# A routed mixture-of-experts stage in parts of 128 rows: eight works of two parts, nine of one with the rows stationary

## The chip, the cores and the metric

One core of a Trainium2 chip runs the whole kernel. The metric is the device time of one launch in microseconds (us), lower is better.

## The reference

A small vision transformer: patch embedding, then two layers of attention and feed-forward, on 32 x 36 = 1152 tokens of 192 features. The change touches the first layer's feed-forward alone, a shared expert for all tokens plus eight routed ones, of which each token takes two:

```
def _expert(xf, W1, W2, W3):                    # 192 -> 768 -> 192
    gate = jnp.minimum(xf @ W1, 10.0)
    up = jnp.clip(xf @ W3, -10.0, 10.0)
    return jax.nn.silu(gate) * up @ W2
scores = jnp.sqrt(jax.nn.softplus(flat @ gate_w))
_, indices = jax.lax.top_k(scores + gate_bias, 2)
weights = take_along_axis(scores, indices); weights /= weights.sum(-1)
y = _expert(flat, w1s, w2s, w3s)                # shared
routed = sum over the two picks of weight * _expert(flat, w1[e], w2[e], w3[e])
```

## The kernel before

**Stages.** Embedding and attention of layer 0 take the first 75 us. Then the shared expert runs in three chunks of 384 tokens (`CHW`), of the third only the first two of six units (`AHEAD`). Now 16 routed works follow, then the rest of the shared expert (the tail, `TAIL`), then layer 1.

**Routing.** VectorE counts each expert's tokens, gives each expert as many works of 256 rows (`WT`) as it needs, and makes a slot for each pick (`bases`, `slots`, L1805 to L1827). GpSimd scatters the rows by indirect DMA into a DRAM array of slots, `marked_rows` (L1479), 18 DMAs. `experts` (L1829) makes the expert number of every work, `eid`, which SyncE loads into a register to address the weights.

**One work.** n counts works; buffers alternate with its parity.

- SyncE loads 1.5 MB of gate and up weights into `stage` (`load_weights`, L375), 0.6 MB of down weights (`load_down`, L384) and 256 rows (`load_rows`, L392). It works through its list in order, each load behind the waits of the ones before it.
- Each fp32 matrix is split into a high and a low part for TensorE's faster format: ScalarE copies the high part of four pieces of 768 columns (L712), then GpSimd subtracts it for three pieces and VectorE for the fourth (`e_split_low`, L728 and L726).
- TensorE transposes the rows (`e_rows`, L701); ScalarE and VectorE split them likewise (L753, L790).
- Gate and up (`e_gate_up`, L665): six units of 128 hidden columns, each 2 matrices x 5 matmuls, the weights stationary and the 256 rows moving. The result has the hidden columns on partitions. ScalarE takes silu (L739), VectorE clips (L760) and multiplies (L767).
- Down (`e_down`, L685): two tiles of 128 rows, six fp32 matmuls each (two instructions per matmul), the hidden values stationary. VectorE copies the tile out (`e_copy`, L805) and GpSimd scatters it home to DRAM, `slots_out` (`send_home`, L1489).

**Order.** Every engine has its own list, written out by hand. TensorE: gate and up of n, row transposes of n+1, down of n-1. GpSimd:

```
for n in range(3, WORKS + 1):
    if n > 4:
        pool.wait_ge(st_y[n % 2], 16 * (n - 4 + n % 2))
    e_split_low(nc.gpsimd, pool, n, n % 2, range(3))
    pool.wait_ge(S0["w_lo"], 4 * n + 3)
    if n > 3:
        send_home(n - 3)
```

The wait on `st_y` is for the landing of the send of work n-4, the one issued at the end of the turn before. When all works are home, SyncE loads them back in token order (`G`, L412), VectorE adds them weighted (L1894), and layer 1's first projection begins (L1074).

Of the kernel before, what the change touches and what calls it, by code (L numbers as in the profile page):

```python
# [5 lines left out]
F32 = mybir.dt.float32  # L6
# [32 lines left out]
WT = 256  # L39

WORKS = (PICKS * TOK - E0) // WT + E0
SLOTS = WORKS * WT
# [11 lines left out]
ZROWS = SLOTS // P // 4  # L54
SPARE = P * ZROWS

# [6 lines left out]
TAIL_AT = ((6, 0), (6, 1), (7, 0))  # L63
TAIL_ADD = ((6, 8, 6), (8, 9, 7))
# [81 lines left out]
def tower(nc, patches, tokw, consts, rows, wa, l1w, wo, moe0w, moe0d, moe1w, xs, ys, out):  # L146
    xs = nc.dram_tensor("marked_rows", (SLOTS, XW1), F32, kind="Internal").ap()
    ys = ys.rearrange("w s d -> (w s) d")
    with ExitStack() as ctx:
# [57 lines left out]
        base = sb("base", [P, E0])  # L207
        slot = sb("slot", [P, TILES * E0])
# [4 lines left out]
        eidf = sb("eidf", [P, WORKS])  # L213
        eid = sb("eid", [P, WORKS], I32)

# [3 lines left out]
        with r1a:  # L219
# [8 lines left out]
            XR = [sb(f"XR{b}", [P, WT // P, 256 + 1], F32, r1a) for b in range(4)]  # L228
            XWh = [sb(f"XWh{b}", [P, 2 * WT], F32R, r1a) for b in range(2)]
            XWl = [sb(f"XWl{b}", [P, 2 * WT], F32R, r1a) for b in range(2)]  # L230
            YO = [sb(f"YO{b}", [P, WT // P, D], F32, r1a) for b in range(2)]
# [65 lines left out]
        r_own, r_sel, r_pos, r_idx, r_eid = (sem("r_" + s) for s in ("own", "sel", "pos", "idx", "eid"))  # L297
        zeroed, zero_set, scattered = sem("zeroed"), sem("zero_set"), sem("scattered")
        ld_w2 = [sem(f"ld_w2{b}") for b in range(2)]
        ld_x = [sem(f"ld_x{b}") for b in range(4)]  # L300
# [36 lines left out]

        block = ctx.enter_context(nc.Block())
# [4 lines left out]
        def _(sp):  # L343
# [17 lines left out]
            for j in range(4):  # L361
                sp.dma_start(xz[:, j * ZROWS * XW1:(j + 1) * ZROWS * XW1],
                             zero[:].rearrange("p r d -> p (r d)")).then_inc(zeroed, 16)
# [4 lines left out]
            def load_weights(n):  # L368
# [5 lines left out]
                experts[n] = sp.value_load(eid[0:1, n - 1:n], min_val=1, max_val=E0)  # L374
# [3 lines left out]
            def load_down(n):  # L378
                if n >= 2:
                    sp.wait_ge(S["down_ready"], 9 + 2 * (n - 2))  # L380
# [6 lines left out]
            def load_rows(n):  # L387
                if n > 4:
                    sp.wait_ge(x_T, n - 4)
                    sp.wait_ge(st_y[n % 2], 16 * (n - 4 + n % 2))  # L390
                rows = xs[(n - 1) * WT:n * WT, :].rearrange("(a p) d -> p a d", p=P)
                sp.dma_start(XR[n % 4][:, :, 0:D], rows[:, :, 0:D]).then_inc(ld_x[n % 4], 16)  # L392
                sp.dma_start(XR[n % 4][:, :, D:256 + 1], rows[:, :, P:XW1]).then_inc(ld_x[n % 4], 16)
# [12 lines left out]
            load_down(TAIL)  # L406
            for par in range(2):
                sp.wait_ge(st_y[par], 16 * WORKS)
# [213 lines left out]
        def units(n):  # L622

            return (n + 1) * FC0 + AHEAD

        TAIL_U = units(TAIL) - AHEAD
        TAIL_D = 9 + 2 * WORKS

        def e_operands(n, c, w, cols):
# [5 lines left out]
            else:  # L635
                h, l = XWh[n], XWl[n]
                xpart = [h[:, 0:WT], h[:, 0:WT], l[:, 0:WT], h[:, WT:2 * WT], l[:, WT:2 * WT]]
# [8 lines left out]
        def e_gate_up(pe, u, n, par, c, these=range(MOE0.fc)):  # L646

            width = WT if c is None else CHW
# [4 lines left out]
            for fc in these:  # L653
                if c is not None or (isinstance(n, int) and n == 1 and fc < 2):
                    if not (isinstance(u, int) and u == 0 and fc < 2):
                        pe.wait_ge(S0["silu_ready"], u + (fc - 1))
                elif not (isinstance(n, int) and n == 1 and fc == 2):
                    pe.wait_ge(S0["h_ready"], u + (fc - 2))
                if not (isinstance(u, int) and u == 0 and fc < 2):
# [8 lines left out]
        def e_down(pe, u, qpar, n, par, shared, loaded, these=range(MOE0.fc)):  # L668
# [1552 lines left out]
```

## Time and profile before

| | us |
|---|---|
| median of 3 runs | 566.83 |
| lowest, highest | 561.97, 567.05 |
| span of the profiled execution | 564.3 |

The profile covers one execution; its own time is its span, 564.3 us, 2.5 us under the median. Times inside it count from the span's start. A row of a timeline or chain gives start, duration and what ran; "[x <-y]" behind it is idle time ahead of it and what ended it. Busy time of TensorE (PE) is no measure of its peak: matmuls overlap, so the pitch from one start to the next is what counts, not the mean duration.

### The profile page before, as it was taken

Reading aid. Unit: us, or ns where it says so; the run is one execution under the profiler, and the core shown is the slowest. Engines: PE = TensorE matmul, PEld = TensorE weight load, DVE = VectorE, ACT = ScalarE, POOL = GpSimd, SP = SyncE. Lnnn points to the kernel's source line nnn. Section 1 sums busy time; section 2 is a strip of 40 time slices with the busy share of each in tenths; the row PEclk is TensorE's granted clock in tenths of the full one; section 3 lists DMA queues with packets and bytes.
Section 4 is the critical chain, followed back from the end, with each engine's and each line's share of the span. In section 5 each row is a group of like instructions: output and inputs, shape, how many; then the busy total and the mean of one; then the engine's idle time right before and its main releaser. Section 6 shows DMA issues by size and latency. Waiting matters only on the chain.

```text
span 564.3 us, 9739 instructions
## 1 busy us (share of the span) xinstructions
PE 518.0 (92%) x3430; PEld 493.6 (87%) x3430; DVE 376.2 (67%) x892; ACT 256.7 (45%) x531; POOL 230.4 (41%) x194
## 2 busy tenths in 40 slices
PE   5799896989999999999999979998996889999996
PEld 5798895989999999999999869786775789999995
DVE  1665848756666666656664587699977765566665
ACT  0337463315544555445543234984750463254331
POOL 1403100746566577656766313486743100041200
PEclk9999959899999999999999989999798799899998
DMA  8750000847465676557662503000201000000001
GB/s 337 259 227 1 2 0 1 314 126 258 144 235 199 225 257 249 196 201 255 216 253 76 189 3 153 2 2 1 77 1 51 28 0 2 2 0 2 1 21 43
DMA packets 22634, 65.03 MB, mean 115 GB/s; under 512 B 6432, under 2 KB 15008, under 8 KB 19776
## 3 DMA queue, kind: packets, MB, share of 16 engines
q1 hardware_dynamic: 20192, 59.55, 29.9%
q0 software_dynamic: 2400, 4.93, 2.5%
q8 instruction: 25, 0.41, 0.3%
q14 instruction: 17, 0.14, 0.1%
HBM read 55.50 MB, written 8.97 MB: 114 GB/s over the span
## 4 chain that ended last, share of the span: by engine, by line
PE 56%; DVE 10%; DMA 4%; POOL 4%; issue 3%; ACT 2%; SPq 0%; DVEq 0%; POOLq 0%; ACTq 0%
PE psum L665 17%; PE psum L448 10%; PE psum L685 10%; PE psum L1074 4%; PE psum L465 4%; PE psum L1106 3%; PE psum L1089 2%; PE psum L472 2%; DMA slots_out<-YO,XR 2%; PE psum L1131 2%; DMA XR<-marked_rows 1%; POOL w0l L728 1%; PE psum L701 1%; POOL w0t L726 1%; DVE OW L2009 1%
## 5 line engine op out<-in xcount | busy, mean ns | idle before, releaser
L728 POOL TENSOR_TENSOR w0l<-stage,w0h 128x768 fp32r<-128x768 f32 x34 | 62.5, 1839 | 81.9 <-ACT w0h L712 69.6
L685 PE MATMUL psum<-w0d,a0h 128*128 128x192 f32 x492 | 84.7, 331 | 1.3 <-DVE a0h L767 1.3
L685 PEld LDWEIGHTS psum<-w0d,a0h 128*128 128x128 f32 x492 | 81.2, 193 | 1.6 <-DVE a0h L767 1.6
L760 DVE TENSOR_SCALAR a0t<-psum 128x256 f32<-128x256 f32 (+1 forms) x114 | 50.8, 445 | 42.6 <-PE psum L665 42.4
L739 ACT ACTIVATE psum<-psum 128x256 f32<-128x256 f32 x96 | 35.3, 368 | 85.3 <-PE psum L665 81.3
L665 PE MATMUL psum<-XWh,w0h 128*128 128x256 f32 x192 | 56.1, 292 | 0.0
L665 PE MATMUL psum<-XWh,w0t 128*128 128x256 f32 x192 | 54.4, 283 | 0.0
L665 PE MATMUL psum<-XWl,w0h 128*128 128x256 f32 x192 | 53.9, 281 | 0.0
L665 PE MATMUL psum<-XWl,w0t 128*128 128x256 f32 x192 | 53.9, 281 | 0.0
L665 PE MATMUL psum<-XWh,w0l 128*128 128x256 f32 x192 | 53.8, 280 | 0.0
L448 PE MATMUL psum<-X,w1h 128*128 128x384 f32 x144 | 50.1, 348 | 1.5 <-DVE a1hf L603 1.5
L767 DVE SCALAR_TENSOR_TENSOR a0h<-psum,a0t 128x256 f32<-128x256 f32 x96 | 40.8, 425 | 10.0
L543 ACT ACTIVATE a1s<-psum 128x384 f32<-128x384 f32 x36 | 17.6, 491 | 55.2 <-PE psum L448 55.2
L726 POOL TENSOR_TENSOR w0t<-stage,w0t 64x768 fp32r<-64x768 f32 x20 | 36.8, 1839 | 9.7 <-ACT w0t L712 7.1
L603 DVE TENSOR_TENSOR a1hf<-psum,a1s 128x384 f32<-128x384 f32 x36 | 20.0, 557 | 28.9 <-ACT a1s L543 28.8
L465 PE MATMUL psum<-d,a1hh 128*128 128x384 f32 x108 | 35.2, 385 | 3.2 <-DVE a1hl L567 1.9
L448 PE MATMUL psum<-X,w1t 128*128 128x384 f32 x144 | 37.6, 342 | 0.0
L665 PEld LDWEIGHTS psum<-XWh,w0h 128*128 128x128 f32 x192 | 36.3, 189 | 0.0
L665 PEld LDWEIGHTS psum<-XWh,w0t 128*128 128x128 f32 x192 | 36.2, 189 | 0.0
L665 PEld LDWEIGHTS psum<-XWh,w0l 128*128 128x128 f32 x192 | 36.1, 188 | 0.0
L665 PEld LDWEIGHTS psum<-XWl,w0h 128*128 128x128 f32 x192 | 36.1, 188 | 0.0
L665 PEld LDWEIGHTS psum<-XWl,w0t 128*128 128x128 f32 x192 | 36.1, 188 | 0.0
(261 smaller groups left out, 1290.8 us busy)
## 6 DMA issues: line engine op xcount, KB each, us to landing
stage<-moe0w SPq DMA_DIRECT2D x18, 1536.0 KB, 7.2
w0d<-moe0d SPq DMA_DIRECT2D x18, 576.0 KB, 3.9
stage<-moe1w SPq DMA_DIRECT2D x4, 1056.0 KB, 4.9
marked_rows<-zero SPq DMA_DIRECT2D x4, 772.0 KB, 13.1
patch<-patches SPq DMA_DIRECT2D x4, 768.0 KB, 8.1
XR<-marked_rows SPq DMA_DIRECT2D x16, 192.0 KB, 3.5
G<-slots_out SPq DMA_DIRECT2D x6, 288.0 KB, 4.4
XR<-marked_rows SPq DMA_DIRECT2D x16, 65.0 KB, 3.7
```

Of the source, the lines that this page charges most:

```text
L448: last = nc.tensor.matmul(bank[bk][:, 0:CHW], wt, x, start=(i == 0), stop=(i == 4))
L465: return nc.tensor.matmul(bank[4 + d % 4][:, 0:2 * D], A["hh"][q][:, fc, cols], w["d"][:, fc, :, :].rearrange("p a d -> p (a d)"), start=( ...
L543: nc.scalar.activation(A["s"][par][:], bank[par][:, 0:CHW], ACT.Silu).then_inc(S["silu_ready"], 1)
L603: nc.vector.tensor_tensor(A["hf"][par][:], bank[2 + par][:, 0:CHW], A["s"][par][:], ALU.mult).then_inc(S["h_ready"], 1)
L665: last = nc.tensor.matmul(bank[b][:, 0:width], w, x, start=(i == 0), stop=(i == 4))
L685: last = nc.tensor.matmul(dst, A0["h"][qpar][:, fc, t * P:(t + 1) * P], W0[par]["down"][:, fc, :], start=(fc == these[0]), stop=(fc == the ...
L726: ins = engine.tensor_tensor(dst, src[64:P], dst.bitcast(F32), ALU.subtract)
L728: ins = engine.tensor_tensor(W0[par]["l"][:, mat, :], src, W0[par]["h"][:, mat, :].bitcast(F32), ALU.subtract)
L739: nc.scalar.activation(e_silu(fc, width, routed), bank[gate_bank(fc, routed)][:, 0:width], ACT.Silu).then_inc(S0["silu_ready"], 1)
L760: nc.vector.tensor_scalar(A0["t"][fc % 2][:, 0:width], bank[2 + fc % 2][:, 0:width], LIMIT, -LIMIT, ALU.min, ALU.max).then_inc(S0["clip_re ...
L767: nc.vector.scalar_tensor_tensor(out=A0["h"][qpar][:, fc, 0:width], in0=e_silu(fc, width, width == WT), scalar=SILU_LIMIT, in1=A0["t"][fc ...
L1074: last = nc.tensor.matmul(bank[(2 * g + half) % 6][0:GW, 0:L1H], x, w, start=(i == 0), stop=(i == 4))
```

## The change

The routed rows are cut into parts of 128 (`PARTS` is 25). Even works (`WIDE`, eight) take two parts of one expert as before, odd works (`LONE`, nine) take one; they alternate, lone first, 17 works in all. A lone work keeps its rows stationary and streams the weights in halves of 384 columns (`e_rows_gate_up`); what comes out has rows on partitions, so TensorE turns it in two sets of three transposes (`e_turn`), which ScalarE copies out (`e_turned`). GpSimd splits all four pieces of a lone work and two of a wide one, VectorE the other two. Weights are loaded two works ahead. VectorE makes the expert and the first part of each work (`wide_parts`, `lone_parts`, `experts`, `places`), and SyncE loads the part number into a register too (`part`, with the semaphore `r_part`). The loops over works are unrolled.

```
-WT = 256
-WORKS = (PICKS * TOK - E0) // WT + E0
+WT = P
+PARTS = (PICKS * TOK - E0) // WT + E0
+WIDE = E0
+LONE = PARTS - 2 * WIDE
+WORKS = WIDE + LONE
...
             load_weights(1)
             load_down(1)
             load_weights(2)
+            load_weights(3)
+            sp.wait_ge(r_part, 1)
             sp.wait_ge(scattered, 16 * PICKS * TILES)
             load_rows(1)
             load_rows(2)
+            load_down(2)
             for n in range(2, WORKS + 1):
-                if n > 2:
-                    load_rows(n)
-                load_weights(n + 1)
-                load_down(n)
+                if n < WORKS:
+                    load_rows(n + 1)
+                if n + 2 <= TAIL:
+                    load_weights(n + 2)
+                load_down(n + 1)
...
+        def e_rows_gate_up(pe, u, n):
+            pe.wait_ge(x_lo, n)
+            for half in range(2):
...
+                for mat in range(2):
+                    pe.wait_ge(S0["w_lo"], n * 4 + 2 * (mat + 1))
+                    for i, (x, w) in enumerate(e_operands(1, None, W0[1], (slice(0, P), mat,
+                                                                           slice(half * LH, (half + 1) * LH)))):
+                        last = nc.tensor.matmul(bank[2 * mat + half][:, 0:LH], x, w, start=(i == 0), stop=(i == 4))
+                last.then_inc(S0["gu_ready"], 1)
+
+        def e_turn(pe, u, n, half):
+            pe.wait_ge(S0["h_ready"], u + (half + 1))
+            if half:
+                pe.wait_ge(h_out, turned_in(n) - 1)
+            for k in range(3):
+                last = nc.tensor.transpose(bank[7][:, k * P:(k + 1) * P], hR[:, half * LH + k * P:half * LH + (k + 1) * P],
+                                           ident)
+            last.then_inc(h_T, 1)
...
+            for n in range(1, WORKS + 1):                      # TensorE
+                u = units(n)
+                if n % 2:
+                    e_rows_gate_up(pe, u, n)
+                    if n < WORKS:
+                        e_rows(pe, n + 1)
+                    e_turn(pe, u, n, 0)
+                    if n > 1:
+                        e_down(pe, units(n - 1), 0, n - 1, 0, False, loaded(n - 1))
+                        e_turn(pe, u, n, 1)
                 else:
+                    e_gate_up(pe, u, n, 0, None, range(1))
+                    if n == 2:
+                        e_turn(pe, units(1), 1, 1)
+                    e_gate_up(pe, u, n, 0, None, range(1, FC0))
+                    e_rows(pe, n + 1)
+                    e_down(pe, units(n - 1), 1, n - 1, 1, False, loaded(n - 1))
+            e_gate_up(pe, TAIL_U, TAIL, 0, 2, range(AHEAD, AHEAD + 1))
+            e_down(pe, units(WORKS), 1, WORKS, 1, False, loaded(WORKS))
+            e_gate_up(pe, TAIL_U, TAIL, 0, 2, range(AHEAD + 1, FC0))
+            e_down(pe, TAIL_U, 0, TAIL, 0, True, loaded(TAIL), range(AHEAD, FC0))
...
+            for n in range(1, WORKS + 1):                      # ScalarE
+                u = units(n)
+                if n % 2:
+                    if n > 1:
+                        e_split_next(act, n + 1, 0)
+                        e_split_next(act, n + 1, 1)
+                    e_rows_silu(act, u, 0)
+                    if n > 1:
+                        e_split_next(act, n + 1, 2)
+                    e_rows_silu(act, u, 1)
+                    if n > 1:
+                        e_split_next(act, n + 1, 3)
+                    if n < WORKS:
+                        e_rows_high(act, n + 1, units(n))
+                    e_turned(act, n, 0)
+                    if n > 1:
+                        e_turned(act, n, 1)
+                else:
+                    if n > 2:
+                        e_split_next(act, n + 1, 0)
+                    e_act(act, u, 2 * WT, these=range(1))
+                    if n == 2:
+                        e_turned(act, 1, 1)
+                        e_split_next(act, 3, 0)
+                    for fc in range(1, FC0):
+                        e_split_next(act, n + 1, fc) if fc < 4 else None
+                        e_act(act, u, 2 * WT, these=range(fc, fc + 1))
+                    e_rows_high(act, n + 1, units(n))
...
-            for n in range(3, WORKS + 1):
+            for n in range(3, TAIL + 1):                       # GpSimd
                 if n > 4:
-                    pool.wait_ge(st_y[n % 2], 16 * (n - 4 + n % 2))
-                e_split_low(nc.gpsimd, pool, n, n % 2, range(3))
-                pool.wait_ge(S0["w_lo"], 4 * n + 3)
+                    pool.wait_ge(st_y[n % 2], sent(n - 4))
+                parts = 4 if n % 2 else 2
+                e_split_low(nc.gpsimd, pool, n, n % 2, range(parts))
+                pool.wait_ge(S0["w_lo"], 4 * n + parts)
                 if n > 3:
                     send_home(n - 3)
...
-            experts()
             e_product(dve, 0, 0, 5, CHW)
-            e_dve(dve, FC0, 1, CHW, None, None, None)
+            e_dve(dve, FC0, 1, CHW, None, {1: wide_parts, 2: lone_parts, 3: experts})
             e_split_low(nc.vector, dve, 1, 1)
+            places()
             prior()
             share(sc, E0, comb[:], True)
             weights()
...
+            e_rows_low(dve, 1)
+            e_split_low(nc.vector, dve, 2, 0, (0, 1))
...
+            for n in range(1, WORKS + 1):                      # VectorE
+                u = units(n)
+                if n % 2:
+                    if n > 2:
+                        dve.wait_ge(h_T, turned_in(n - 2))
...
+                    for half in range(2):
+                        e_rows_product(dve, u, half)
+                else:
+                    e_dve(dve, u, 0, 2 * WT, downs(n - 2))
+                if n < WORKS:
+                    e_rows_low(dve, n + 1)
+                if n % 2 and n > 1:
+                    e_split_low(nc.vector, dve, n + 1, 0, (2, 3))
+                if n > 1:
+                    e_copy(dve, n - 1)
+            e_dve(dve, TAIL_U, 0, CHW, downs(WORKS - 1), these=range(AHEAD, FC0 - 1))
+            e_copy(dve, WORKS)
+            e_dve(dve, TAIL_U, 0, CHW, None, these=range(FC0 - 1, FC0))
```

## Rows read from the trace of the kernel before

**Rows 1.** The page's engine shares: busy time, share of span, instructions.

```profile
PE 518.0 (92%) x3430; PEld 493.6 (87%) x3430; DVE 376.2 (67%) x892; ACT 256.7 (45%) x531; POOL 230.4 (41%) x194
```

**Rows 2.** The chain that ended last, steady stretch: start, us, what ran.

```profile
202.24 3.90 PE psum L685 x24
206.15 7.12 PE psum L665 x60
213.26 0.44 PE psum L701 x4
```

**Rows 3.** Busy time by stretch: engines, TensorE's clock, DMA share, GB/s.

```profile
148.80:298.10 149.30, 149.17 (x1146) 148.97 (x1145) 97.03 (x208) 75.58 (x143) 97.58 (x66) 1.00 0.65 229
```

**Rows 4.** GpSimd's timeline through one work.

```profile
208.62 1.84 POOL L728 TENSOR_TENSOR w0l<-stage,w0h 128x768 fp32r<-128x768 f32 x1 [3.14 <-ACT w0h L712]
...
212.60 1.83 POOL L728 TENSOR_TENSOR w0l<-stage,w0h 128x768 fp32r<-128x768 f32 x1
214.71 0.99 POOL L1489 DMA_INDIRECT slots_out<-YO,XR  x1 [0.28 <-POOL w0l L728]
216.00 0.96 POOL L1489 DMA_INDIRECT slots_out<-YO,XR  x1 [0.31 <-issue]
```

**Rows 5.** The chain in layer 1: ten matmuls, rows stationary, 396 columns moving.

```profile
336.21 1.80 PE psum L1074 x10
```

**Rows 6.** Landings: all sends; those of 297.8, 299.1; SyncE there; scatter of 101.7.

```profile
slots_out<-YO,XR POOLq DMA_INDIRECT x32, 2.3
...
L1489 POOL DMA_INDIRECT slots_out<-YO,XR x2: 957/958/959, 297.8 to 299.1; - x2
...
DMA to landing us min/median/max: 4.3/4.4/4.6
...
298.35 0.36 SPq L384 DMA_DIRECT2D w0d<-moe0d  x1
...
DMA to landing us min/median/max: 7.0/7.0/7.0
```

**Rows 7.** SyncE's timeline: one steady turn, the first weight load, its landing.

```profile
206.31 0.36 SPq L384 DMA_DIRECT2D w0d<-moe0d  x1
...
208.56 0.35 SPq L375 DMA_DIRECT2D stage<-moe0w  x1
...
99.97 0.35 SPq L375 DMA_DIRECT2D stage<-moe0w  x1
...
DMA to landing us min/median/max: 8.6/8.6/8.6
```

**Rows 8.** VectorE's timeline in the opening: expert numbers, first and last split, what follows.

```profile
98.77 0.17 DVE L1837 TENSOR_SCALAR eid<-eidf 128x16 int32<-128x16 f32 x1
...
103.08 0.56 DVE L760 TENSOR_SCALAR a0t<-psum 128x384 f32<-128x384 f32 x1 [1.40 <-PE psum L665]
...
109.58 0.96 DVE L728 TENSOR_TENSOR w0l<-stage,w0h 128x768 fp32r<-128x768 f32 x1
...
112.76 0.97 DVE L726 TENSOR_TENSOR w0t<-stage,w0t 64x768 fp32r<-64x768 f32 x1
...
117.50 1.02 DVE L796 TENSOR_TENSOR H<-psum,H 128x384 f32<-128x384 f32 x2
```

**Rows 9.** ScalarE's timeline in a work: one weight copy.

```profile
207.65 0.84 ACT L712 ACTIVATE w0h<-stage 128x768 fp32r<-128x768 f32 x1
```

**Rows 10.** TensorE before work 1: timeline, clock of that stretch, chain to work 2.

```profile
125.57 0.66 PE L701 MATMUL psum<-const,XR 128*128 128x128 f32 x4 [2.08 <-DMA XR<-marked_rows]
...
126.20:129.60 3.40, 3.40 (x14) 3.40 (x12) 1.25 (x2) 3.33 (x5) 1.82 (x1) 0.50 0.95 309
...
133.85 10.68 PE psum L665 x90
```

**Rows 11.** The chain at the end: last send, first projection of layer 1.

```profile
315.23 2.32 DMA slots_out<-YO,XR
330.18 5.37 PE psum L1074 x20
```

More of the change, by code:

```diff
@@ L207, in tower @@
         base = sb("base", [P, E0])
+        twos = sb("twos", [P, E0])
+        rest = sb("rest", [P, E0])
+        ends = sb("ends", [P, 2, 2, E0])
+        shift2 = sb("shift2", [P, 2, E0])
+        order = sb("order", [P, 2, LONE])
+        place = sb("place", [P, 2, LONE])
+        held = sb("held", [P, 2, LONE])
+        part = sb("part", [P, 2, LONE], I32)
         slot = sb("slot", [P, TILES * E0])
@@ L296, in tower @@
         rt1_z, rt1_b, rt1_p = sem("rt1_z"), sem("rt1_b"), sem("rt1_p")
-        r_own, r_sel, r_pos, r_idx, r_eid = (sem("r_" + s) for s in ("own", "sel", "pos", "idx", "eid"))
+        r_own, r_sel, r_pos, r_idx, r_eid, r_part = (sem("r_" + s) for s in ("own", "sel", "pos", "idx", "eid", "part"))
         zeroed, zero_set, scattered = sem("zeroed"), sem("zero_set"), sem("scattered")
         ld_w2 = [sem(f"ld_w2{b}") for b in range(2)]
-        ld_x = [sem(f"ld_x{b}") for b in range(4)]
+        ld_x = [[sem(f"ld_x{b}{i}") for i in range(RING3)] for b in range(2)]
+        h_T, h_out = sem("h_T"), sem("h_out")
         marked, copied, numbered = sem("marked"), sem("copied"), sem("numbered")
@@ L679, in e_down @@
                     dst = bank[e_bank(t)][:, 0:D]
[L680 removed]
+                    if n == 1:
                         pe.wait_ge(S0["acc_done"], len(SHARED_ADD))
[L682 to L683 removed]
+                    elif t == 0:
+                        pe.wait_ge(y_done, copies(n - 1) if n % 2 == 0 else copies(n - 2) + 1)
+                    elif n > 2:
+                        pe.wait_ge(y_done, copies(n - 2))
                 for fc in these:
[L685 removed]
+                    h = hT[:, fc, :] if lone else A0["h"][qpar][:, fc, t * P:(t + 1) * P]
+                    last = nc.tensor.matmul(dst, h, W0[par]["down"][:, fc, :],
                                             start=(fc == these[0]), stop=(fc == these[-1]))
@@ new lines, in _, with reached @@
+            lone_to, wide_to, lone_from, wide_from = (ends[:, i, k, :] for i in range(2) for k in range(2))
+            grid = [P, 2, LONE, E0]
+            def reached(to, side):
+                return nc.vector.tensor_tensor(
+                    to.rearrange("p (k w e) -> p k w e", k=2, e=E0),
+                    counts[:, 0:LONE].unsqueeze(1).unsqueeze(3).to_broadcast(grid),
+                    ends[:, side].unsqueeze(2).to_broadcast(grid), ALU.is_ge)
+            above, within = (rk[i][:, 0:2 * LONE * E0] for i in range(2))
@@ new lines, in wide_parts, with lone_parts @@
+            def wide_parts():
+                k0 = rk[0][:, 0:E0 * FULL].rearrange("p (e k) -> p e k", k=FULL)
+                own.link(nc.vector.tensor_reduce(twos[:], k0[:, :, 1:FULL:2], AX.X, ALU.add))
+                earlier(wide_from, twos[:])
+                own.link(nc.vector.tensor_tensor(wide_to, wide_from, twos[:], ALU.add))
+                own.link(nc.vector.tensor_scalar(ends[:, :, 1, :], ends[:, :, 1, :], float(WIDE), None, ALU.min))
+            def lone_parts():
+                own.link(nc.vector.tensor_tensor(twos[:], wide_to, wide_from, ALU.subtract))
+                own.link(nc.vector.scalar_tensor_tensor(out=rest[:], in0=twos[:], scalar=-2.0, in1=works[:],
+                                                        op0=ALU.mult, op1=ALU.add))
+                earlier(lone_from, rest[:])
+                own.link(nc.vector.tensor_tensor(lone_to, lone_from, rest[:], ALU.add))
```

304 lines of the change are left out of this document (160 added, 144 removed).

## The prediction

> **What bounds the kernel now.** I read the page's engine shares first, then the chain of waits, then the timelines of the routed stretch engine by engine. The page says TensorE is busy 92% of the span and GpSimd 41% [rows 1]; those are averages, and the change touches only the stretch from about 125 to 330 us. There the chain repeats one pattern: 7.12 us of gate/up matmuls (60 of them, one every 0.119 us), 0.44 us for four transposes, 3.90 us of down matmuls (24 instructions, 0.163 us each), then the next work: 11.46 us in all [rows 2]. Over 148.8 to 298.1 us TensorE never rests and its granted clock is 1.00, its 2.4 GHz level [rows 3]. So today a routed work costs 11.46 us, and a pair 22.92 us, all TensorE.
>
> The second thing to see is how little room GpSimd has. Its three weight splits start 1.99 us apart (208.62 to 212.60 in two steps) and run 1.83 us, the first send starts 0.28 us after them, the second 1.29 us later, and this second send lands 2.3 us after it starts [rows 4]. Before its next splits GpSimd waits for exactly that landing (the wait on st_y for work n-4, whose send stands right before it). One work therefore needs 3 x 1.99 + 0.12 + 1.29 + 2.3 = 9.7 us on GpSimd, of 11.46. It waits for ScalarE's copy only in the remainder.
>
> **TensorE's own sum.** A lone work has 2 halves x 2 matrices x 5 matmuls, 20 with 384 moving columns. The nearest row, also rows stationary and weights moving (396 columns), is ten in 1.80 us [rows 5]; I take 0.176 us each, 3.5 us. Its two row transposes are 0.22 us, its six turning transposes 0.66 us, its one down tile 1.95 us. A wide work stays 11.46 us. A pair is 11.46 + 3.5 + 0.22 + 0.66 + 1.95 = 17.8 us against 22.92: 5.1 us less for each of eight pairs, 41 us in all, less about 6 us for the seventeenth work. If TensorE stayed the bound this would be the gain. It won't stay the bound.
>
> **GpSimd's sum.** The weights of 17 works and the tail must still be split, whatever the number of rows. In a pair GpSimd takes four pieces of the lone work, two sends of the wide one, the wait for their landing, two pieces of the next wide work, one send, and its landing. From the first piece: last piece ends at 3 x 1.99 + 1.83 = 7.80; second send starts at 7.80 + 0.28 + 1.29 = 9.37; it lands L2 later; two pieces 3.82; the single send starts 0.28 later, at 13.57 + L2; it lands L1 later; 0.1 to restart. The loop is 13.67 + L1 + L2. With both at 2.3 it is 18.3 us, already above TensorE's 17.8. The same loop passes through VectorE: the wide work's pieces 2 and 3 wait there for GpSimd's two, 1.06 us each (four from 109.58 to 113.73) [rows 8], and TensorE's wide work waits for them. In the lone phase TensorE now waits some 2 to 4 us in each pair.
>
> **What the sends land in is the disputed price.** Before, sends mostly go out with no load starting: 2.3 us. Two didn't. Those of 297.8 and 299.1 us stand 0.55 us before and 0.73 us after SyncE's down load of 298.35, and landed in 4.6 and 4.3 us; and a scatter of 101.7 us, with 1.5 MB weight loads queued, took 7.0 [rows 6]. After the change, the lone work's fourth piece ends 8 to 10 us after the wide work's first matmul (call that G). The two sends go out at about G+9 and G+10. SyncE issues the next down load when the lone down matmuls end, at G + 7.12 + 0.22 + 1.95 = G+9.3: the spacing of the 4.3 and 4.6 rows. I take L2 = 4.5 (ends 2.3 and 7.0). The single send goes out near G+19. The wide work's down matmuls end at G+17.5, which releases another down load; the weight load before it is issued at G+12.4 (SyncE's turn from down load to weight load lasts 2.3 us [rows 7], the new register load adds some 0.7) and takes 7 us. I take L1 = 3.4, the middle of 2.3 and 4.6. So a pair is 13.67 + 4.5 + 3.4 = 21.6 us, only 1.3 below before.
>
> **Other engines in a pair.** ScalarE: eight copies of 0.84 [rows 9], eight silus, two turned copies and two row copies, none over 0.6: about 12 us. VectorE: eight clip and product pairs of some 1 us, two splits and five copies, about 12 us. Both hide. Behind VectorE's wait for GpSimd's pieces stand the copies of the wide work before; their send comes half a pair later, so that costs nothing. The weights arrive 7 us after SyncE's issue and are wanted 7 us or more after it; 5 MB in 21.6 us is 230 GB/s, what rows 3 already show. The turn's waits (h_T, h_out) stand behind down matmuls of 3.90 us and cost nothing; without that cover each would cost 0.5 us of ScalarE copy.
>
> **The opening.** The expert numbers move from before VectorE's last product of chunk 0 (98.8 us) to behind the fourth unit of chunk 1. VectorE's idle of 1.4 us ahead of the third unit [rows 8] hides wide_parts (five instructions of about 0.2), lone_parts makes the next clip 0.6 late, experts follow at about 106.5: eid at 107.4 instead of 98.9. SyncE's load takes 1.0 us to issue and 8.6 to land [rows 7]: 117.0. VectorE's four splits of work 1 then end at 122.1 instead of 113.7 [rows 8]. Behind them on VectorE queue places (eleven small instructions, 2.9 us, to 125.0), prior, share and weights (3.75, from 113.73 to 117.50 before; to 128.8), three additions (1.6, to 130.4) and two clip and product pairs of chunk 2 (2.3, to 132.7). Rows of work 1 need r_part and a register load, and stand behind the load of work 3 that SyncE now issues first, so they land about 131, when the third addition also frees the bank. TensorE's down matmuls of chunk 2 start at 132.8 and take 3.8 (before they had the 1.2 GHz level, granted clock 0.50, after an idle of 2.1 us [rows 10]; now the idle is some 7). The lone work runs 136.6 to 140.1; silu, product and row split (0.3 + 0.5 + 0.56 + 0.69) let work 2 start at 142.3. Before it started at 133.85 + 3.56 = 137.4 [rows 10]: 4.9 us lost. I can't bound this tightly: 0 to 8.
>
> **The first pair** has no send to wait for: TensorE's 17.8 plus 0.95 because ScalarE's second copy for work 3 stands behind silu and the turned copy. 18.75 us.
>
> **The closing.** The tail's first unit waits for the eighteenth split. Then one unit 1.75, down of work 17 1.95, two units 3.5, the product 1.38 behind them, and only then the copy of work 17 (0.36), since VectorE's order puts it behind three tail units: 8.95. Before, the last send starts at 315.23 and the first projection of layer 1 at 330.18 [rows 11], 14.95 later. Together 24.0 us. The half clock after TensorE's stall adds 1.7 (four units, 3.4 us at half rate). What follows 330.18 is the same as before.
>
> **The sum.** Work 2 at 142.3, the first pair 18.75, seven pairs of 21.6 = 151.2 (the seventh ends where the tail starts), closing 24.0 + 1.7: 337.95 us, against 330.18, so 7.8 us later. The profiled span of 564.3 becomes 572.1. The listed runs' median is 2.5 above that span; I carry this excess over: 574.6.
>
> On the half clock: the row of 126.2 to 129.6 us shows 0.50 after a 2.1 us idle [rows 10]. In each pair TensorE would idle as long, so the clock will fall there too. It costs nothing while GpSimd is the bound. The Trainium skill ("TensorE: Matmul & The Clock Gate", HAM oscillation) warns of just such a loop, a wait per iteration that brings the clock down each time; the trace of before has no such loop and can't show it. By that rule each stall would cost TensorE up to 1.7 us, which changes the sum only where TensorE is the bound.
>
> **Rivals.** *Sends land free.* If the landings stay 2.3, the loop is 18.3 and the pair TensorE's 18.75. 142.3 + 8 x 18.75 + 24.0 = 316.3, 13.9 earlier: 552.9. For it: the median of all 32 sends is 2.3 us. Against it: the two that met a fresh load [rows 6]. It decides at a pair of 20.5, where the time equals that of before. The Trainium skill ("DMA: Bandwidth & Descriptors", queues, rings and completion order) says that each DMA engine goes round-robin between queue rows and switches at packet boundaries. By that with small packets a send would hardly be held, and this rival's 552.9 would come out; with a load's whole share as one packet it would wait the load out, which the 4.6 us row looks like. *Only the wide sends are held.* L1 = 2.3 and L2 = 4.5 is that pair of 20.5: 142.3 + 18.75 + 7 x 20.5 + 25.7 = 330.2, no change, 566.8. *A send waits out a whole 1.5 MB load.* L2 = 7.0 as the scatter, pair 24.1: 355.4, 25 later, 592. Against it: the weight load is issued at G+12.4, after the sends, unless GpSimd runs late.
>
> **How the numbers follow.** Forecast 0.40 (568 to 580 by its ends of the opening and L1); wide sends only 0.20 (561 to 569); free 0.27 (549 to 558); whole load 0.11; something else 0.02. Within 1% (5.7 us, about what a measurement of this kernel can tell from no change) fall 0.2 and a quarter of the forecast's: 0.29. Faster 0.29, slower 0.42. The range takes in the free case and stops short of the last: 551 to 586. The forecast's own range is 568 to 580.
>
> **What would show it.** Wide works starting 21 to 22 us apart; GpSimd's splits waiting on slots_out; sends landing at 4 to 5 us; TensorE idle 2 to 4 us before each wide work, with the granted clock below 1; lone gate/up in 3.5 us; work 2 near 142; last send some 9 us behind the tail's first matmul. Pairs of 18.8 with sends at 2.3 would prove me wrong.

## The result and the profile after

The changed kernel takes 582.1 us (median of four runs, 580.1 to 583.8) against 564.5 for the kernel before: ratio 1.031, interval 1.027 to 1.036. Forecast was 574.6, slower, inside 551 to 586: the sign was right, the loss of 7.8 us was 17.6. Of the almost 10 us between the two losses, 7.5 are the changed kernel's; the other 2.4 come from the kernel before, whose median with a fourth run is 564.5 and not 566.8. Some runs come out a few per cent longer; the ratios, here and in the table of experiments, leave these out and compare with runs of the kernel before made beside them, so they are not quotients of the medians shown. The profiled execution has a span of 580.2 us and lies 0.1 us from its median; its sum below can be laid beside the forecast's term by term.

The chain of waits, from work 2 to work 4 and on (start, us, what). It answers to rows 2.

```profile
141.56 1.43 PE psum L727 x10
...
153.07 3.48 DMA XR<-marked_rows
156.55 0.04 issue
156.60 0.66 PE psum L798 x4
157.25 0.33 PE psum L752 x3
157.58 3.90 PE psum L780 x24
161.48 0.33 PE psum L752 x3
161.81 3.53 PE psum L727 x30
...
173.15 3.22 DMA XR<-marked_rows
...
177.40 3.90 PE psum L780 x24
181.31 0.33 PE psum L752 x3
181.63 3.88 issue
185.52 9.51 PE psum L727 x60
```

Where one kind of step was repeated without a gap before [rows 2], two holes stand now. The row transposes of the next wide work (L798) wait for rows that are still in flight, and before four of the seven wide gate/ups from work 4 to work 16 (those of works 6, 10, 12 and 16) TensorE is idle for 0.5 to 5.2 us, called issue. That name says only that the profile has no releaser. GpSimd's timeline of the same stretch has it:

```profile
170.26 1.83 POOL L826 TENSOR_TENSOR w0t<-stage,w0t 64x768 fp32r<-64x768 f32 x1
172.37 0.99 POOL L1614 DMA_INDIRECT homes<-YO,XR  x1 [0.28 <-POOL w0t L826]
173.66 0.96 POOL L1614 DMA_INDIRECT homes<-YO,XR  x1 [0.30 <-issue]
179.54 1.80 POOL L828 TENSOR_TENSOR w0l<-stage,w0h 128x768 fp32r<-128x768 f32 x1 [4.92 <-DMA homes<-YO,XR]
181.49 1.80 POOL L826 TENSOR_TENSOR w0t<-stage,w0t 64x768 fp32r<-64x768 f32 x1
183.57 1.64 POOL L1614 DMA_INDIRECT homes<-YO,XR  x1 [0.28 <-POOL w0t L826]
```

The second wide send starts at 173.66 and GpSimd goes on 5.88 us later. VectorE's two differences for the same work wait for GpSimd's two:

```profile
183.39 0.96 DVE L828 TENSOR_TENSOR w0l<-stage,w0h 128x768 fp32r<-128x768 f32 x1 [4.96 <-POOL w0t L826]
184.46 0.96 DVE L826 TENSOR_TENSOR w0t<-stage,w0t 64x768 fp32r<-64x768 f32 x1
```

TensorE starts at 185.52, behind them. From the start of the second send to its next difference GpSimd takes 5.9, 4.6, 4.4, 7.0, 4.9, 4.2 and 3.1 us in the seven pairs, mean 4.9; six single sends land 3.0 to 4.6 us after they start, mean 3.5. The waits between 160 and 300 us (line waited for: us in total, times, longest) and the stretches (PE, PEld, DVE, ACT, POOL busy, granted clock, DMA share, GB/s):

```profile
POOL w0l L828 <- DMA homes<-YO,XR: 34.0, 10, 6.0
PEld psum L798 <- DMA XR<-marked_rows: 12.5, 6, 2.7
```

```profile
181.63:185.52 3.89, 0.01 (x2) 0.04 (x1) 1.99 (x3) 1.33 (x2) 3.30 (x2) 0.79 0.60 186
185.52:195.03 9.51, 9.51 (x62) 9.51 (x63) 4.79 (x12) 4.09 (x8) 7.18 (x4) 0.73 0.49 177
161.81:317.81 156.00, 130.79 (x893) 126.11 (x892) 77.14 (x160) 76.28 (x140) 101.78 (x63) 0.95 0.65 218
```

Against [rows 3], TensorE is busy 130.8 of 156.0 us instead of all of it: 3.6 us idle in each pair, where the forecast said 2 to 4. In two of the seven wide gate/ups, behind idle times of 3.9 and 5.2 us, the granted clock is 0.73 and the matmuls take 9.5 us instead of 7.1. The end, against [rows 11]:

```profile
317.81 3.57 PE psum L727 x10
321.38 3.23 PE psum L780 x12
324.61 3.51 PE psum L727 x20
...
329.28 0.36 DVE YO L920
...
330.39 2.33 DMA homes<-YO,XR
...
345.68 4.59 PE psum L1181 x13
```

### The profile page after: what moved, and what is told of

The parts are those of the page before. It is cut to its first block, busy times and chain, and to the rows that moved or that the text cites. A ratio compares the mean times of both kernels' runs of the same rounds, so it can differ in the third digit from the quotient of the medians.

```text
span 580.2 us, 8867 instructions
## 1 busy us (share of the span) xinstructions
PE 495.6 (85%) x3086; PEld 463.8 (80%) x3086; DVE 354.6 (61%) x852; ACT 255.7 (44%) x524; POOL 226.5 (39%) x187
## 4 chain that ended last, share of the span: by engine, by line
PE 65%; DVE 14%; DMA 8%; issue 6%; ACT 4%; SPq 2%; POOL 1%; DVEq 0%; POOLq 0%; ACTq 0%
PE psum L727 14%; PE psum L780 11%; PE psum L505 10%; DMA XR<-marked_rows 4%; PE psum L1181 4%; PE psum L522 3%; PE psum L947 3%; PE psum L1196 3%; PE psum L1213 3%; PE psum L968 2%; PE psum L1028 2%; PE psum L1238 2%; PE psum L529 2%; DVE Y L1731 1%; DMA stage<-moe0w 1%
## 5 line engine op out<-in xcount | busy, mean ns | idle before, releaser
L600 ACT ACTIVATE a1s<-psum 128x384 f32<-128x384 f32 x36 | 17.6, 490 | 54.7 <-PE psum L505 54.7
L727 PE MATMUL psum<-XWh,w0h 128*128 128x256 f32 x96 | 29.0, 302 | 12.2 <-issue 11.0
L809 ACT ACTIVATE w0h<-stage 128x768 fp32r<-128x768 f32 x38 | 31.9, 839 | 11.0 <-DMA stage<-moe0w 10.8
L1614 POOL DMA_INDIRECT homes<-YO,XR x25 | 29.0, 1159 | 17.2 <-DVE YO L920 10.6
L727 PE MATMUL psum<-X,w0h 128*128 128x384 f32 x72 | 28.7, 399 | 7.7 <-DVE w0t L826 2.9
L1213 PEld LDWEIGHTS psum<-VW,AT 108*108 108x108 f32 x264 | 28.9, 184 | 5.4 <-issue 4.7
L1196 PE MATMUL psum<-XB 96*108 96x432 f32 (+1 forms) x88 | 30.0, 487 | 2.6 <-DVE AT L2206 2.6
L809 ACT ACTIVATE w0t<-stage 128x768 fp32r<-128x768 f32 x38 | 31.7, 835 | 0.0
L839 ACT ACTIVATE psum<-psum 128x256 f32<-128x256 f32 x48 | 17.6, 367 | 29.2 <-PE psum L727 28.9
L727 PEld LDWEIGHTS psum<-XWh,w0h 128*128 128x128 f32 x96 | 19.4, 202 | 13.6 <-issue 12.2
L1213 PE MATMUL psum<-VW,AT 108*108 108x112 f32 (+2 forms) x264 | 29.0, 269 | 0.9 <-issue 0.9
```

Of the source, the lines that this page charges most:

```text
L727: last = nc.tensor.matmul(bank[b][:, 0:width], w, x, start=(i == 0), stop=(i == 4))
L809: nc.scalar.activation(W0[par]["t" if two else "h"][:, mat, :], W0[par]["stage"][:, (2 * mat + two) * F0:(2 * mat + two + 1) * F0], ACT.Co ...
L839: nc.scalar.activation(e_silu(fc, width, routed), bank[gate_bank(fc, routed)][:, 0:width], ACT.Silu).then_inc(S0["silu_ready"], 1)
L1196: last = nc.tensor.matmul(bank[b][0:GW, at * GW:(at + c1 - c0) * GW], kT1[g % 2][:, half, :], qT1[g % 2][:, half, c0:c1, :].rearrange("p c ...
L1213: last = nc.tensor.matmul(bank[1 + h // HH][0:GW, h % HH * 3 * HD:h % HH * 3 * HD + n], AT[g % 2][:, h, :], VW[g // 2 % 2][:].rearrange("p ...
L1614: nc.gpsimd.indirect_dma_start(out=ys, out_offset=bass.IndirectOffsetOnAxis(ap=to[:, t, 256:257].bitcast(I32), axis=0), in_=YO[n % 2][:, t ...
```

## Experiments

Below, "first pair" is from work 2's first gate/up matmul to work 4's, "pair" the mean of the seven from there to the tail's, both from TensorE's timeline. In the changed kernel they are 20.0 and 22.3 us (20.25 and 22.3 by the chain, which begins work 4 at 161.81). "Tail to last send" is the time from the tail's first matmul to the start of the last send. Theory 1 says that GpSimd's waits for landings set the pair; theory 2 that the late rows do.

| run | us | ratio to before, interval | work 2 | first pair | pair | tail to last send |
|---|---|---|---|---|---|---|
| changed | 582.1 | 1.031 [1.027, 1.036] | 141.6 | 20.0 | 22.3 | 12.6 |
| again_changed (one run) | 578.0 | – | 140.6 | 19.9 | 22.5 | 9.8 |
| e1_piece0_first | 565.5 | 1.005 [1.000, 1.010] | 143.9 | 20.3 | 20.1 | 9.8 |
| e2_rows_early | 584.0 | 1.036 [1.028, 1.045] | 145.0 | 18.7 | 23.3 | 9.8 |
| e3_both | 563.0 | 1.000 [0.995, 1.005] | 141.5 | 18.7 | 20.5 | 9.8 |
| e4_no_down_loads | 560.2 | 0.995 [0.989, 1.000] | 145.8 | 18.9 | 19.6 | 9.8 |
| e5_copy_sooner | 578.0 | 1.021 [1.015, 1.026] | 143.4 | 19.8 | 22.6 | 6.8 |
| e6_rows_first | 579.9 | 1.027 [1.020, 1.034] | 140.0 | 19.9 | 22.5 | 11.2 |
| e8_four_edits_and_order | 562.8 | 0.994 [0.990, 0.998] | 139.2 | 18.7 | 21.0 | 5.2 |
| e9_vector_takes_64 | 552.8 | 0.978 [0.972, 0.985] | 139.5 | 20.1 | 19.2 | 5.2 |
| e10_loads_behind | 580.4 | 1.030 [1.022, 1.038] | 139.9 | 19.9 | 23.3 | 9.8 |
| e11_spread_differences | 540.2 | 0.960 [0.956, 0.965] | 137.3 | 19.2 | 18.6 | 5.2 |
| e12_swap_alone | 560.8 | 0.997 [0.993, 1.000] | 138.4 | 21.4 | 20.0 | 9.7 |

**e1_piece0_first.** GpSimd's loop:

```diff
+                parts = 4 if n % 2 else 2
+                e_split_low(nc.gpsimd, pool, n, n % 2, range(1))
                 if n > 4:
                     pool.wait_ge(st_y[n % 2], sent(n - 4))
-                parts = 4 if n % 2 else 2
-                e_split_low(nc.gpsimd, pool, n, n % 2, range(parts))
+                e_split_low(nc.gpsimd, pool, n, n % 2, range(1, parts))
```

> GpSimd's wait for the landing of its sends stands behind its first difference of 128 partitions instead of before it, so 1.80 us of work goes under each of the waits. Theory 1 (the landings set the pair: 13.67 us of GpSimd's work plus two waits): up to 1.8 us less for each of the 16 waits after work 1, a pair of 19.5 to 20.5 us instead of 22.3, the program 12 to 25 us below the 582.1 of the changed kernel. Theory 2 (the rows of the next wide work, issued behind the down load in SyncE's list, set it, TensorE's pair 19.9 us): the wide works already start at 19.9 to 22.3 us, so at most the part above 19.9 goes, and nothing if the down load alone sets it: 0 to 3 us less.

16.6 us less for one wait moved behind one instruction; by the two profiles 15.4 of it lies in the seven pairs. GpSimd's timeline there:

```profile
194.84 0.96 POOL L1614 DMA_INDIRECT homes<-YO,XR  x1 [0.30 <-issue]
195.86 1.82 POOL L828 TENSOR_TENSOR w0l<-stage,w0h 128x768 fp32r<-128x768 f32 x1
200.47 1.81 POOL L826 TENSOR_TENSOR w0t<-stage,w0t 64x768 fp32r<-64x768 f32 x1 [2.78 <-DMA homes<-YO,XR]
```

The send takes as long to land as before, but 1.8 us of it is covered; of the 34.0 us of waits 11.3 are left in the same window. The wait is kept ahead of GpSimd's differences of 64 partitions; the first of 128 now runs beside the transfer. Neither kind reads or writes what is sent, and no run drops the wait with the work left on GpSimd, so whether it could go altogether isn't shown. Theory 1 holds as the cause of the pair of 22.3. The pair stops at 20.1 us, which is TensorE's sum with the wait for rows (17.8 + 2), and the chain between 184 and 226 us runs through the row loads at each turn. So theory 2 names what comes next; e3 shows that it isn't alone there.

**e2_rows_early.** SyncE's list, rows loaded two works ahead:

```diff
+            load_rows(3)
             load_down(2)
             for n in range(2, WORKS + 1):
-                if n < WORKS:
-                    load_rows(n + 1)
+                if n + 2 <= WORKS:
+                    load_rows(n + 2)
```

> Rows of work 3 are loaded up front and in the loop those of two works ahead, so they land before the row transposes need them; GpSimd's waits stay. Theory 2 (late rows set the pair): TensorE's stop of 2 us before the row transposes of a wide work goes and with it up to 2 us a pair, 10 to 16 us in all. Theory 1 (GpSimd's waits set it): the stop moves from before the row transposes to before gate and up, the pair stays at 22.3 and the time within 3 us of 582.1.

No gain. No wait for rows is left in the steady stretch, and the first pair, which has no landing to wait for, falls to 18.7: the forecast's 18.75. In the others the idle moves to before gate/up (GpSimd still waits 38.2 us in 10 times). Theory 2 is right for the first pair and wrong for the rest.

**e3_both.** Both edits.

> The first two edits together. Theory 1: as the first alone, 12 to 25 us below 582.1, with a further 0 to 3 us. If both walls stand close to each other (TensorE with late rows 19.9, GpSimd 21 to 22): the first alone stops at a pair of 19.9, both together reach 18 to 19, so that the two together give 5 to 8 us more than the first alone.

563.0, first pair 18.7, but the pair is 20.5, not 18 to 19. GpSimd still waits for landings (15.0 us in 8 times), and ScalarE waits longer for stage loads (20.3 us in 11, against 9.0 in 7). Early rows brought nothing beyond the first pair: with them away, the chain runs through a stage load of 9.3 us and through idle times of 2.8 to 3.6 us before the wide gate/up.

**e4_no_down_loads.** Down weights from work 3 on aren't reloaded (4 of 1536 columns are moved), so this run leaves out a part of the work:

```diff
+                cols = 4 if n > 2 else MOE0.fc * D
-                sp.dma_start(W0[n % 2]["down"].rearrange("p a b -> p (a b)"), ...
+                sp.dma_start(W0[n % 2]["down"].rearrange("p a b -> p (a b)")[:, 0:cols], ...
```

> Leaves out the reload of the down weights from work 3 on (4 columns of 1536 are moved, all waits stay). If these 0.75 MB transfers are what GpSimd's sends queue with, the landings of the wide works' second sends fall from 4 to 7 us to 2.3 to 3.0, two landings a pair together from about 8.2 to 5.3, and under theory 1 the pair falls by about 2.5 to 3 us and the program by 18 to 25 us. If the stage loads (1.5 MB) are what they meet, the landings stay at 4 to 7 us and the program within 5 us of 582.1; rows then also land sooner only by the time of the down load before them.

With the waits in their old places the pair falls by 2.7 us:

```profile
POOL w0l L829 <- DMA homes<-YO,XR: 21.2, 12, 2.1
```

A wait is 1.8 us instead of 3.4, and from the start of a wide work's second send GpSimd goes on after 2.9 us on average (2.4 to 3.1) instead of 4.9. So the down load is what makes a good part of the landings long, as the forecast read from the two sends at 297.8 and 299.1 [rows 6]. (The down load is 0.56 MB, not the 0.75 that the expectation says.) Rows land sooner too, in 2.5 us instead of 3.5, so part of the gain may be theirs.

**e5_copy_sooner.** VectorE's end:

```diff
-            e_dve(dve, TAIL_U, 0, CHW, downs(WORKS - 1), these=range(AHEAD, FC0 - 1))
+            e_dve(dve, TAIL_U, 0, CHW, downs(WORKS - 1), these=range(AHEAD, AHEAD + 1))
             e_copy(dve, WORKS)
-            e_dve(dve, TAIL_U, 0, CHW, None, these=range(FC0 - 1, FC0))
+            e_dve(dve, TAIL_U, 0, CHW, None, these=range(AHEAD + 1, FC0))
```

> Only the closing: VectorE copies the last work's rows (line 920) behind the first of the tail's units instead of behind three of them. If the copy's place in VectorE's list sets the last send, the stretch from the tail's start to the last send's issue falls from 12.6 us to 7 to 9 and the program by 4 to 5 us to 577 to 578. If it is the tail's own work at half clock that sets the end, the send goes out sooner and the first projection of the next layer starts as long after the tail's start as before (27.9 us): 582.

578.0, in the expected range. The last send goes out 6.8 us behind the tail's start (12.6), with the down matmuls partly at the low clock again (granted clock 0.70):

```profile
321.14 2.54 PE psum L727 x10
323.68 3.08 PE psum L780 x12
...
326.85 0.37 DVE YO L920
...
327.97 2.33 DMA homes<-YO,XR
...
343.04 2.28 PE psum L1181 x6
```

From the tail to layer 1 it is 21.9 us instead of 27.9. Not all of that shows in the total, since in this execution the tail begins 3.3 us later. Nor is all of it the edit's. The changed kernel's second execution, without an edit, has the full clock there (start, us, what):

```profile
317.88 2.02 PE psum L727 x10
319.90 1.95 PE psum L780 x12
321.85 3.51 PE psum L727 x20
...
342.70 2.61 PE psum L1181 x7
```

That is 24.8 us from the tail to layer 1, as in six other profiles with the old order (24.8 to 24.9), and 20.1 to 20.3 in e8, e9 and e11, which have this edit and the full clock. The place of the copy is worth 4.6 us; the rest belongs to the clock of one execution.

**e6_rows_first.** `load_weights(3)` moves behind `load_rows(2)` in SyncE's opening.

> Only the opening: SyncE issues the third stage load behind the rows of works 1 and 2 instead of ahead of them. If that 1.5 MB load is what makes work 1 late, work 2 starts 1 to 3 us before the 141.56 of the changed kernel and the program is at 578 to 582; if the expert numbers and the shared expert's last matmuls set it, nothing changes (582), and the lone work 3 gets its weights later: up to 585.

Work 2 at 140.0, 1.6 us sooner, and 579.9. e5, whose opening is the changed kernel's (143.4), and the changed kernel's second execution (140.6) say that a microsecond or two of work 2's start is scatter: what this edit brings isn't shown.

**e8_four_edits_and_order.** e3, e5, e6, and in SyncE's loop `load_weights(n + 2)` ahead of `load_rows(n + 2)`.

> The first two edits, the sooner copy, the later third stage load, and in SyncE's loop the stage load ahead of the rows (rows are loaded a work earlier, so they can wait). With the first two alone the pair is 20.2 us (141.47 to 303.34) and the chain's new step is the stage load, issued 3.0 us after the down matmuls that free the down buffer. If the load's late issue is the wall, the pair falls to 18.6 to 19.5 us, and with the closing's 5 us the program reaches 545 to 555; if GpSimd's landings are still the wall, the pair stays at 20 and the program at 556 to 562.

562.8. The closing keeps its gain (5.2 us to the last send), the pair doesn't fall (21.0). The load's late issue wasn't the wall; GpSimd waits for landings 19.3 us in 6 times.

**e9_vector_takes_64.** Besides, the 64-partition differences go to VectorE:

```diff
-                parts = 4 if n % 2 else 2
-                e_split_low(nc.gpsimd, pool, n, n % 2, range(1))
-                if n > 4:
-                    pool.wait_ge(st_y[n % 2], sent(n - 4))
-                e_split_low(nc.gpsimd, pool, n, n % 2, range(1, parts))
-                pool.wait_ge(S0["w_lo"], 4 * n + parts)
+                e_split_low(nc.gpsimd, pool, n, n % 2, (0, 2))
+                pool.wait_ge(S0["w_lo"], 4 * n + 3)
...
                         e_rows_product(dve, u, half)
+                        if half == 0 and n > 1:
+                            e_split_low(nc.vector, dve, n + 1, 0, (1,))
...
-                    e_dve(dve, u, 0, 2 * WT, downs(n - 2))
+                    t_part = lambda i, n=n: e_split_low(nc.vector, dve, n + 1, 1, (i,))
+                    e_dve(dve, u, 0, 2 * WT, downs(n - 2),
+                          {1: lambda: t_part(1), 5: lambda: t_part(3)} if n < WORKS else {})
...
-                    e_split_low(nc.vector, dve, n + 1, 0, (2, 3))
+                    e_split_low(nc.vector, dve, n + 1, 0, (3,))
```

> As the one before, and VectorE makes all differences of 64 partitions (0.96 us each there, 1.84 on GpSimd), GpSimd those of 128. GpSimd then has four differences and three sends a pair (about 12 us) and waits for no landing at all. If GpSimd and its landings are the wall, TensorE's own sum becomes it: a pair of 17.8 to 18.5 us, 535 to 547 for the program. If the stage loads (9 us from issue to landing and 5 to 8 us of splitting for each of two buffers) are the wall, the pair stays at 18.5 to 20 and this run gives within 3 us what the one before gives. If VectorE's two more differences delay its products, the wide gate and up get longer than 7.1 us.

No landing is waited for, and the pair falls to 19.2: 552.8, 2.2% under the kernel before. Two things in its trace can keep it above TensorE's 17.8: VectorE's extra 0.96 us makes the wide gate/up 7.7 to 8.8 us long, and a lone work's stage buffer goes round in 18.7 (load 9.35, last difference 9.2 behind its landing).

**e12_swap_alone.** The changed kernel with only that exchange, its rows, opening and closing as they were.

> The changed kernel with one edit: VectorE makes the differences of 64 partitions and GpSimd those of 128, so GpSimd waits for no landing. Rows, copy and opening stay as they were. Theory 1 with the late rows as the next wall (TensorE's sum with the wait for rows 19.8 to 19.9 us a pair): pair 19.9 to 20.5 and 558 to 565 for the program. If the landings alone were the wall and the rows hide: the pair of the version with all edits, 19.1, and 555 to 558.

560.8, pair 20.0: 17.8, rows 1.4, and the longer gate/up. One exchange of engines is worth 21 us and brings the program level with before. In the profiles, 22.5 us apart, 15 of it lie in the eight pairs; work 2 starts 3.2 us sooner, which this edit doesn't touch, and the closing is 3.1 us shorter, as it is in the changed kernel's second execution.

**e10_loads_behind.** In the opening, `load_weights(2)` stands behind `load_rows(1)` and `load_weights(3)` behind `load_rows(2)`.

> Only the opening: the second stage load too is issued behind the rows of work 1, so that 2.1 MB instead of 3.6 or 5.2 MB are in flight from 105 us on. In the changed kernel TensorE's down matmuls of the shared expert stop for 0.3 to 2.1 us again and again from 109 to 120 us and end at 129, while the loads run. If the amount in flight makes these stops, they end by about 114 us, the down matmuls end by 122 and the rows of work 1 land sooner by the same 2 to 4 us; work 2 then waits for its own stage load (issued at about 121, landed 130, split by 136 to 138) and starts at 137 to 140 instead of 141.56, 576 to 580 for the program. If the stops have another cause they stay, and work 2 starts at 140 to 144.

TensorE's stops at 109 to 120 us are gone (busy 10.00 us of the 10 between 109 and 119), and work 2 starts at 139.9. By itself this points to the loads in flight. But e12 and e11, with as many in flight (390 and 382 GB/s), have no stops either.

**again_changed.** No edit.

> The changed kernel once more, unedited. TensorE's stops at 109 to 120 us stood in seven profiles of it and its variants (3.2 to 5.9 us busy of the 10 between 109 and 119) and not in three (10.00 of 10), two of which have the same loads in flight. If they belong to the program, they stand here in the same place (TensorE busy 3 to 5 us of those 10) and work 2 starts at 141 to 142; if they belong to the single execution, they may be missing, and work 2 then starts 2 to 4 us sooner. The pairs stay at 22 to 22.7 us, the landings at 3 to 7.

The same window in the two executions of the same program:

```profile
109.00:119.00 10.00, 3.94 (x10) 1.64 (x8) 5.48 (x10) 3.53 (x5) 6.45 (x7) 0.66 0.95 379
```

```profile
109.00:119.00 10.00, 10.00 (x64) 10.00 (x63) 2.50 (x4) 3.04 (x4) 7.63 (x8) 1.00 1.00 363
```

The stops belong to the execution. (The expectation counts seven profiles with them; by the same window there are nine: the changed kernel's first and those of e1 to e9.) The tail starts at 317.9 in one and 317.8 in the other, so they don't explain the loss. What causes them stays open.

**e11_spread_differences.** e9, with the two differences between a clip and its product:

```diff
-                          {1: lambda: t_part(1), 5: lambda: t_part(3)} if n < WORKS else {})
+                          mid={2: lambda: t_part(1), 4: lambda: t_part(3)} if n < WORKS else {})
```

> The fastest version so far (pair 19.1 us, 552.8) with VectorE's two differences for a lone work placed between a clip and its product (third and fifth unit) instead of behind a product (second and sixth). The lone works' stage buffer goes round in 18.7 us there (load 9.3, then the last difference 9.2 us after its landing, behind the sixth unit), and the wide gate and up takes 7.7 to 8.8 us instead of 7.1. If these two set the pair, it falls by about 1 us to 18.0 to 18.5 and the program to 544 to 549; if something else does, it stays within 2 us of 552.8.

540.2 us, 4.0% under the kernel before, the fastest here. VectorE's timeline and the routed stretch:

```profile
198.04 0.42 DVE L871 TENSOR_SCALAR a0t<-psum 128x256 f32<-128x256 f32 x1
198.49 0.96 DVE L827 TENSOR_TENSOR w0t<-stage,w0t 64x768 fp32r<-64x768 f32 x1
199.48 0.42 DVE L878 SCALAR_TENSOR_TENSOR a0h<-psum,a0t 128x256 f32<-128x256 f32 x1
```

```profile
156.55:286.54 129.99, 127.40 (x895) 123.29 (x894) 88.56 (x175) 74.32 (x139) 81.12 (x49) 1.00 0.73 257
```

TensorE's next unit waits for the clip of this unit, which frees its PSUM bank, but for the product of the unit before only, so the product can wait. The pair is 18.6, 0.6 us less and not the expected 1, TensorE is busy 127.4 of 130.0 us at the full clock, and GpSimd falls from 101.8 to 81.1 us. Of the 11.0 us between the spans of e9 and e11, 7.5 lie before the tail. 2.1 of them lie before work 2, where e9 has the stops of 109 to 120 us and e11 has not; 5.4 lie in the eight pairs, and only these can be put down to the edit. The other 3.5 lie behind the tail, where both have the same code, and aren't explained.

## Why the prediction was right in its sign and short in its size

The terms add up: 7.7 us too little at the first projection of layer 1 (345.68 against 337.95), 0.4 behind it. Two of the forecast's own sums are rounded up by 0.1 to 0.15 us: work 2 adds up to 142.15 and the closing without the clock to 23.9.

| term | forecast | measured | difference |
|---|---|---|---|
| work 2 starts | 142.3 | 141.56 | -0.7 |
| first pair | 18.75 | 20.25 | +1.5 |
| seven pairs | 151.2 | 156.0 | +4.8 |
| closing | 25.7 | 27.87 | +2.2 |

**TensorE's own sum** had its lone gate/up right (3.49 to 3.53 us for 20) and missed a step. The half-length lone phase pulled the rows of the next wide work, which stand behind the down load in SyncE's list, into TensorE's path: down load, register load, two row loads, landing 3.5 us after issue, 2 us of idle. The sum with rows is 19.9, not 17.8. That is the first pair's 1.5 us (e2: 18.7 once the rows are early), and hidden in the seven others by GpSimd's waits (e2: no gain). Of TensorE's 25.2 us idle in these seven, 10.6 stand before the row transposes and 11.0 before gate/ups. By this sum the rival "sends land free" would have given some 19.9 a pair, not 18.75. No run has free sends; the nearest is e12, where GpSimd waits for no landing: 20.0, with a longer wide gate/up.

**GpSimd's sum** was the right mechanism with a term too small. The loop is 13.67 + L1 + L2; L2 was taken as 4.5 and measured 4.9, L1 as 3.4 and measured 3.5: 22.1 of the 22.3 us. That is 0.5 us of the 0.7 a pair. The sum had no term for ScalarE's copies, on which GpSimd waits for 0.7 and 0.3 us in two of the seven pairs, and which outlast the landing of two single sends. I had taken the spacing of two rows; now the landings scatter from 2.3 to 6.8 (8.3 in the second execution), and a mean over that tail lies above the row that looks nearest. What they land in was right in the main: without the down loads a wait falls from 3.4 to 1.8 us (e4). The second send starts 2.2 us behind the down load and 0.7 us ahead of a stage load (171.49, 173.66, 174.32), and no run takes the stage load away.

**The rivals.** Free sends, and only wide sends held (20.5), are out by the landings, the whole-load case by its size: one send of 7.0, not all. The Trainium skill ("DMA: Bandwidth & Descriptors", queues, rings and completion order) says that a DMA engine switches between queue rows at packet boundaries. The prediction's reading of it for small packets, a send hardly held, disagrees with landings of 3 to 7 us here. Its other reading, a load's whole share as one packet, isn't shown either: e4 shows that the down load makes the waits longer, not by what mechanism.

**The half clock costs nothing while GpSimd is the bound**: this held for the pairs. The pair that begins with the gate/up of 9.51 us is no longer than the rest (22.1), since GpSimd paces it. That the clock falls in each pair did not come true: it fell in two of the seven, behind idle times of 3.9 and 5.2 us, and not behind 1.4 and 0.5. In the closing TensorE is the bound, and I gave the half clock 1.7 us: the first unit and the down matmuls took 6.80 us instead of 3.7, so 3.1, and in the second execution of the same program 3.7: this term was a matter of the execution. The Trainium skill ("TensorE: Matmul & The Clock Gate", HAM oscillation) warns of a loop whose waits bring the clock down each time. The trace agrees in part: it came down in some of the turns, 0.95 granted over the stretch, and cost nothing there.

**The closing**: besides the clock, the copy behind three tail units was named and costed; undisturbed it is 9.8 us where I had 8.95, since 0.7 us lies between the copy's end and the send. Without the low clock the whole closing is 24.8 us, against 24.0 forecast; with the low clock 27.9, against 25.7. The copy's place is worth 4.6 us (e5).

**The opening** came out right in its total, with its parts off: the expert numbers were ready at 104.2, not 107.4, and in the profiled execution the stops let the shared expert's down matmuls end at 129.2 (119.6 in the second one, where the rows of work 1 end an idle of 6.7 us at 129.8, close to the forecast's 131). Work 2 starts only 1.0 us apart in the two, because the late rows of work 1, which were in the sum, cover most of it.

**VectorE and ScalarE hide**: right, but the forecast stopped there. VectorE was busy 77 of the 156 us of seven pairs, so it had 11 us of slack in each, and it does in 0.96 us what GpSimd does in 1.84. Half of the 42 us between the changed kernel and e11 comes with that exchange alone (e12).

## What to carry to other kernels

When a change halves the work of the bounding engine in half of the steps, write out the loop of each other engine with the waits in it, and then the queue that issues each load: ask of every DMA in it what it stood behind and how much of the vanished time had hidden it. A wait for an engine's own transfer is paid in full by an in-order engine; put independent work between the transfer and the wait, or give the work that stands behind the wait to an engine that has none. Where an instruction must be squeezed into a producer's turn, put it behind the step that frees the other engine's buffer, not behind the last.

## What the runs showed of the hardware that was not expected

- The same 64x768 difference takes 0.96 us on VectorE and 1.83 on GpSimd, and 128x768 takes as long as 64x768 on each (0.97 and 1.84).
- At 379 GB/s, TensorE's down matmuls stopped for 0.2 to 2.1 us again and again in one execution (busy 3.94 us of 10), while ScalarE and VectorE were late too and GpSimd was not; in another execution of the same program, at 363 GB/s, they ran through. The kernel before ran through the same 10 us at 244 GB/s. Nine of the thirteen profiles of the changed kernel and its variants have the stops (3.2 to 5.9 us busy); the cause is open.
- After two wide sends 1.3 us apart, issued some 1 and 2 us behind a 0.56 MB load, GpSimd went on 4.9 us after the start of the second on average; most sends before landed in 2.3. With that load taken away it was 2.9 us (e4).
